# A state scan written as 64 explicit steps over 2048 columns, in place of a scan instruction over rows of time

## The reference

```python
delta = jax.nn.softplus(jnp.einsum('blr,dr->bld', delta_lo, dt_proj_w) + dt_proj_b)
A = -jnp.exp(A_log)
...
def step(h, inp):
    dt, bt, ct, xt = inp
    dA = jnp.exp(dt[..., None] * A)
    h = dA * h + dt[..., None] * bt[:, None, :] * xt[..., None]
    y = jnp.einsum('mdn,mn->md', h, ct)
    return (h, y)
h0 = jnp.zeros((M, Dm, STATE), dtype=x.dtype)
_, ys = jax.lax.scan(step, h0, (dt_seq, b_seq, c_seq, x_seq))
...
return jnp.einsum('bld,od->blo', y + x * D, out_proj_w)
```

## Time and profile before

| | us |
|---|---|
| median of 3 runs (lowest, highest) | 1664.71 (1663.49, 1667.7) |
| span of the profiled execution | 1666.7 |
| preparation of the scan stage | 1016.6 to 1069.0 of the span |
| the 32 units and the last projection | 1069.0 to 1517.2 |
| stage f and the store | 1517.4 to 1666.7 |

### The profile page before, as it was taken

The page is one execution under the profiler, slowest core; times in us unless marked ns, Lnnn a source line. Parts: engine busy times, 40 slices in busy tenths (PEclk is TensorE's granted clock), DMA queues, the critical chain, the costliest instruction groups (busy, mean ns, idle before and its releaser), DMA issues.

```text
span 1666.7 us, 41395 instructions
## 1 busy us (share of the span) xinstructions
PE 1383.1 (83%) x16240; PEld 952.6 (57%) x16240; DVE 1227.1 (74%) x2009; ACT 988.0 (59%) x2218; POOL 488.0 (29%) x423
## 2 busy tenths in 40 slices
PE   4889995799999987889999997477777777876998
PEld 2667773344444435566666774365566666664676
DVE  5787766777777747886674544699999999995533
ACT  4667672276666675766674444666666666652433
POOL 2756656712221004745551004304410000000000
PEclk8999998699999998999999999678877878776999
DMA  4100000000000001000000000201000000000000
GB/s 139 59 18 1 0 1 1 1 1 2 1 0 1 1 1 39 31 34 0 0 1 1 1 0 19 76 3 41 19 26 4 3 4 4 3 3 1 1 0 25
DMA packets 21070, 23.56 MB, mean 14 GB/s; under 512 B 2880, under 2 KB 15696, under 8 KB 20560
## 3 DMA queue, kind: packets, MB, share of 16 engines
q1 hardware_dynamic: 20912, 21.25, 4.0%
HBM read 17.04 MB, written 4.19 MB: 13 GB/s over the span
## 4 chain that ended last, share of the span: by engine, by line
PE 56%; DVE 20%; issue 12%; ACT 8%; POOL 2%; DVEq 0%; SPq 0%; DMA 0%; ACTq 0%; POOLq 0%
PE ps L517 12%; PE ps L770 7%; PE ps L594 7%; PE ps L604 7%; PE ps L801 6%; PE ps L709 4%; PE ps L672 4%; DVE arena L1643 3%; PE ps L692 3%; DVE maxima L1565 3%; DVE arena L1629 2%; DVE xn L1366 2%; ACT hr L951 2%; ACT arena L951 1%; PE ps L645 1%
## 5 line engine op out<-in xcount | busy, mean ns | idle before, releaser
L1055 ACT ACTIVATE arena<-ps,arate 128x128 f32<-128x128 f32 x1024 | 285.3, 383 | 143.5 <-PE ps L770 73.8
L1643 DVE TENSOR_TENSOR_SCAN arena<-arena 128x2048 f32<-128x2048 f32 x64 | 286.0, 4468 | 1.1
L801 PE MATMUL ps<-arena 128*32 128x32 f32 x8192 | 167.0, 236 | 82.8 <-DVE arena L1643 57.9
L1565 DVE TENSOR_REDUCE maxima<-ps 128x1 f32<-128x512 f32 (+3 forms) x320 | 190.4, 634 | 59.1 <-PE ps L675 40.0
L770 PE MATMUL ps<-arena 128*128 (+1 forms) x2048 | 203.1, 255 | 30.9 <-issue 15.5
L517 PE MATMUL ps<-xp,wup 128*128 128x512 f32 (+1 forms) x768 | 206.1, 415 | 13.7 <-ACT hr L951 10.0
L517 PE MATMUL ps<-hr,wdn 128*128 128x512 f32 x768 | 200.0, 410 | 10.0 <-DVE hr L1468 7.3
L1309 POOL TENSOR_TENSOR hr<-arena,hr 128x512 fp32r<-128x512 f32 x128 | 174.7, 1371 | 91.1 <-ACT hr L951 90.6
L801 PEld LDWEIGHTS ps<-arena 128*32 128x32 f32 x8192 | 129.6, 133 | 118.0 <-DVE arena L1643 61.2
L1468 DVE TENSOR_TENSOR hr<-arena,hr 128x512 fp32r<-128x512 f32 x128 | 126.4, 1001 | 91.0 <-ACT hr L951 89.1
L1017 ACT ACTIVATE arena<-ps 128x1024 f32<-128x1024 f32 (+1 forms) x192 | 150.4, 812 | 71.5 <-PE ps L692 37.0
(11 more groups left out here) (203 smaller groups left out, 1982.2 us busy)
## 6 DMA issues: line engine op xcount, KB each, us to landing
arena<-up_dram SPq DMA_DIRECT2D x16, 256.0 KB, 2.9
arena<-dn_dram SPq DMA_DIRECT2D x16, 256.0 KB, 3.2
parts_dram<-arena SPq DMA_DIRECT2D x8, 384.0 KB, 2.7
arena<-parts_dram SPq DMA_DIRECT2D x48, 64.0 KB, 2.4
arena<-up_dram SPq DMA_DIRECT2D x1, 1024.0 KB, 4.8
arena<-dn_dram SPq DMA_DIRECT2D x1, 1024.0 KB, 8.3
out_dram<-x SPq DMA_DIRECT2D x1, 1024.0 KB, 5.1
arena<-sel_dram SPq DMA_DIRECT2D x1, 768.0 KB, 5.0
```

The costliest lines, as they stand in the source:

```text
L801: mm = e.matmul(ps[32 * j:32 * j + 32, 6, rb * DQ:(rb + 1) * DQ], cz[:, t, :], h[:, :, t], start=(k == 0), stop=(k == 15), skip_group_chec ...
L1055: ins = e.activation(da[:, dq % 2, r * TR:(r + 1) * TR], ps[:, n % 2, j * TR:(j + 1) * TR], ACT.Exp, scale=arate[:, dq * DQ + r:dq * DQ + ...
L1565: e.tensor_reduce(maxf[:, at_max[0]:at_max[-1] + 1:max(1, at_max[-1] - at_max[0])], ps[:, n % 2, 0:ng * w].rearrange("p (g k) -> p g k", g ...
L1643: ins = e.tensor_tensor_scan(hs[:, par, part], da[:, par, part], hs[:, par, part], 0.0, ALU.mult, ALU.add)
```

## The change

The state is kept for all chunks and channels at once: a partition is still (batch row, state), and the free axis is (16 chunks, 128 channels), W = 2048 columns. The 64 steps of a chunk are walked one by one. In step t:

- TensorE writes the inputs of all columns into PSUM banks 0 to 3: 16 matmuls of 12 rows by 128 columns (`inputs`), an outer product of the bf16 parts of B and u. It also forms four banks of dt times exp(A_log), 8 matmuls of 12 rows by 64 columns each (`spread_bank`), one unit of four steps ahead;
- ScalarE takes `Exp` of each bank, 512 columns in one activation, and writes them with the time index innermost in the reading order, 2048 elements apart in the target (`decay_bank`);
- VectorE multiplies half of the state by the decay (1024 columns, `decay_state`), GpSimd the other half in two pieces of 512, and VectorE adds the inputs from PSUM (1024, 512 and 512 columns, `add_input`);
- TensorE contracts with C, 16 matmuls of 32 weight columns by 128 moving columns (`state_out`).

The scan instruction, the multiplication by B on VectorE and `arate` are gone. All of dt, u and B are now split and sent to DRAM before the steps begin (`store_dt`, `store_u`, `store_b`), and fetched by eighths (`fetch`). The fetched parts use the room of the weights of the relu mixtures, which are loaded a second time near the end of the steps. C is placed by ScalarE, A_log is exponentiated in the attention stage, and y is projected once, after the last step. The loops of the stage are unrolled.

```diff
+                def fetch(k):
+                    for c0, na in RUNS:
+                        for r in range(RG):
+                            rows = slice(32 * r + 2 * c0, 32 * r + 2 * c0 + 2 * na)
+                            sp.dma_start(dtsf[k % 2][rows], scratch["dt"][k, 0:na, :, GD * r:GD * (r + 1)].rearrange(
+                                "a b d n -> (a b) (d n)")).then_inc(dt_in[k % 2], 16)
...
+                sp.wait_ge(SC["u_split"], 4)
+                store_u(0)
+                sp.wait_ge(parts_out, 16 * (2 * NC + 3))
+                fetch(0)
+                for k in range(1, NC):
+                    store_dt(k)
+                    store_u(k)
+                sp.wait_ge(parts_out, 16 * 5 * NC)
+                fetch(1)
...
+        def spread_bank(e, n):
...
+            if q == 0 and th == 0:
+                e.wait_ge(dt_in[k % 2], 16 * KR * (k // 2 + 1))
+            if n >= 2:
+                e.wait_ge(SC["decay_ready"], n - 1)
+            for j in range(DBK):
+                mm = e.matmul(ps[:, 4 + n % 2, j * 64:(j + 1) * 64], aw[32 * r:32 * r + KR, g0 + j, :],
+                              dts[k % 2][32 * r:32 * r + KR, g0 + j, :, th * TU:(th + 1) * TU], start=True, stop=True)
...
+            for t in range(NSTEP):
+                todo = [n for n in range(ahead, ahead + (5 if t < 4 else 4)) if n < NUN * BKU]
+                ahead += len(todo)
+                for n in todo[0:1]:
+                    spread_bank(e, n)
+                if t + 1 < NSTEP:
+                    e.wait_ge(SC["added"], 3 * t + 1)
+                    inputs(e, t + 1, (0, 1))
+                for n in todo[1:2]:
+                    spread_bank(e, n)
+                if t + 1 < NSTEP:
+                    e.wait_ge(SC["added"], 3 * t + 2)
+                    inputs(e, t + 1, (2,))
+                for n in todo[2:3]:
+                    spread_bank(e, n)
+                e.wait_ge(SC["added"], 3 * t + 3)
+                if t + 1 < NSTEP:
+                    inputs(e, t + 1, (3,))
+                state_out(e, t)
+                for n in todo[3:]:
+                    spread_bank(e, n)
...
+            to = decay[:, u % 2, :].rearrange("p (t m d) -> p t m d", t=TU, d=D)[:, :, :, d0:d0 + DBK]
+            e.activation(to.rearrange("p t m d -> p d m t"),
+                         ps[:, 4 + n % 2, :].rearrange("p (d m t) -> p d m t", d=DBK, t=TU), ACT.Exp,
+                         scale=-1.0).then_inc(SC["decay_ready"], 1)
...
+                        if t >= 2 and n == 0:
+                            e.wait_ge(SC["y_done"], t - 1)
+                        e.wait_ge(SC["added"], 3 * (t - 1) + 2 + n)
+                        e.tensor_tensor(hs[:, t % 2, cols], decay[:, u % 2, t4 * W + cols.start:t4 * W + cols.stop],
+                                        hs[:, 1 - t % 2, cols], ALU.mult).then_inc(SC["pool_multiplied"], 1)
...
+                if n == 0:
+                    e.wait_ge(SC["multiplied"], t)
+                else:
+                    e.wait_ge(SC["pool_multiplied"], YP * (t - 1) + n)
+                e.tensor_tensor(to, to, of, ALU.add).then_inc(SC["added"], 1)
...
+                if t >= 2:
+                    e.wait_ge(SC["y_done"], t - 1)
+                e.wait_ge(SC["added"], 3 * (t - 1) + 1)
+                e.tensor_tensor(hs[:, t % 2, 0:HALF], decay[:, u % 2, t4 * W:t4 * W + HALF], hs[:, 1 - t % 2, 0:HALF],
+                                ALU.mult).then_inc(SC["multiplied"], 1)
...
+                for t in range(1, NSTEP):
+                    add_input(t, 0)
+                    add_input(t, 1)
+                    if t + 1 < NSTEP:
+                        decay_state(t + 1)
+                    add_input(t, 2)
```

More of the change, by code:

```diff
@@ L45 @@
 RMS_EPS = 1e-6
[L46 to L51, removed]
+NM = S // CHUNK
+NSTEP = CHUNK
+TU = 4
+TC = 8
+NC = NSTEP // TC
+NUN = NSTEP // TU
+W = NM * D
+HALF = W // 2
+RG = 4
+KR = 12
+RUNS = ((0, 3), (3, 2), (5, 1))
+GD = D // RG
+DBK = 512 // (NM * TU)
+BKU = D // DBK
+NPART = 3
+YP = 2
 ARENA = 164 * 256
@@ L188, in build @@
[L188 to L197, removed]
@@ new lines, in inputs @@
+        def inputs(e, t, banks):
+            k = t // TC
+            if t % TC == 0 and 0 in banks:
+                e.wait_ge(u_in[k % 2], 16 * KR * (k // 2 + 1))
+                e.wait_ge(b_in[k % 2], 16 * KR * (k // 2 + 1))
+            for mm_ in range(4):
+                for r in banks:
+                    rows = slice(32 * r, 32 * r + KR)
+                    mm = e.matmul(ps[:, r, mm_ * D:(mm_ + 1) * D], bs[k % 2][rows, mm_, t % TC, :],
+                                  us[k % 2][rows, mm_, t % TC, :], start=True, stop=True)
+            mm.then_inc(SC["in_done"], 1)
@@ new lines, in state_out @@
+        def state_out(e, t):
+            u, t4 = t // TU, t % TU
+            if t4 == 0:
+                e.wait_ge(SC["c_placed"], 2 * u + 2)
+                if u >= 2:
+                    e.wait_ge(SC["yT_ready"], u - 1)
+            for mh in range(4):
+                for ml in range(4):
+                    m = 4 * mh + ml
+                    mm = e.matmul(ps[32 * ml:32 * ml + 32, 6 + u % 2, 0:D], cz[:, u % 2, ml, (4 * mh + t4) * 32:(4 * mh + t4 + 1) * 32],
+                                  hs[:, t % 2, m * D:(m + 1) * D], start=(t4 == 0 and mh == 0),
+                                  stop=(t4 == 3 and mh == 3), skip_group_check=True)
+            mm.then_inc(SC["y_done"], 1)
@@ L899, in run_stages @@
+            state_turn(e, NUN - 1)
+            e.wait_ge(SC["yT_ready"], NUN)
+            for i in range(NT):
+                mm = e.matmul(ps[:, i // TPB, i % TPB * P:(i % TPB + 1) * P], yT[:, i * P:(i + 1) * P], opw[:],
+                              start=True, stop=True)
+                if i % TPB == TPB - 1:
+                    mm.then_inc(SC["proj_done"], 1)
         def run_stages(e, attention, scan, gelu_mixture, relu_mixture):
@@ L1039, in attention_scalar @@
             e.sem_inc(AT["exp_done"], 2)
+            e.activation(alog[:], alog[:], ACT.Exp).then_inc(alog_exp, 1)
             def go(items, u, par, at, first=False):
```

584 lines of the change are left out of this document (296 added, 288 removed).

## The result

The changed kernel takes 1650.3 us (median of 4 runs, 1646.4 to 1653.7) where the kernel before took 1666.2 in the same session: a ratio of 0.989, 95% interval 0.985 to 0.993. It is faster, by 16 us; the forecast was 142 us and a range that ended at 1592. The profiled execution has a span of 1651.6 us.

A forecast was written before the change was run, and what follows sets the result against it. VectorE was taken to bound the scan stage. Start 1092, steps 268, stall 7 and end 8 gave 1375 against 1517.4, 142 us less: 1524 of span, 1522 us forecast, range 1496 to 1592.

The forecast's parts named there:

- TensorE per step, at full clock: In each step, inputs, spreads, state_out and shape changes on TensorE were to take 3.9 us, as much as VectorE.
- rival 3: In the steps, TensorE at half clock: 5.9 to 8.5 us a step, 1695 us at 7.0; chance 0.07.
- The value taken, 0.63 us for 512 columns: ScalarE's decay activations from PSUM in each step: 0.63 us each, no penalty for the scattered store.
- Rival 2: ScalarE's scattered store in the steps: about 1.06 us an activation, 4.6 us a step, 1544 us; chance 0.15.
- The loops of 4.1 us: Three loops in each step, by shared port, VectorE and TensorE, each about 4.1 us; meshing them was taken as 4.25.
- The floor of 3.93: VectorE's four instructions of a step summed, with 0.03 us from one to the next: at least 3.93 us.
- Rival 1: Shared port out of phase: VectorE's product waits up to 1.29 us for GpSimd's, 5.2 us a step, 1582 us; chance 0.12.
- rule on two SBUF inputs: A VectorE instruction with two SBUF inputs and a GpSimd one reading SBUF exclude each other for a whole instruction.
- The start: Preparation before the steps: first VectorE product near 1092, steps starting 23 us later than the units did.
- The 0.45 us an issue: SyncE's time to issue one transfer in the preparation: 0.45 us, so 16.2 us for the first fetch's 36.
- The stall: In step 3, bank 32 waits for the second eighth of dt behind 21 stores: 7 us.
- The end: After the steps: state_out, copies, turn, 16 fp32 projections and the addition, 8 us.

The follow-up runs named there:

- e16: Changed kernel with its scattered store kept, GpSimd's memsets later, spreads and inputs contracting over all 128 rows: 1585.8 us.
- e1: Changed kernel with the decay activation reading PSUM in strides and storing runs of eight neighbouring elements: 1614.2 us, ratio 0.969 to the kernel before.
- e8b: Changed kernel with the dense store, later memsets, and spreads and inputs contracting over all 128 rows: 1546.8 us.
- e19: Changed kernel with dense store, later memsets, u's later stores on GpSimd behind the first spread, and a lead of 68 float32 products: 1587.4 us.
- e10: Changed kernel with dense store, later memsets and four added full-array float32 products a step, one ahead of each spread bank: 1757.3 us.
- e9: Changed kernel with the dense store and GpSimd's memsets started only after the stage's statistics: 1608.9 us.

## Why the prediction was wrong

The direction was right; the size was not, and the range missed by 58 us. The span came out at 1651.6 where the sum gave 1524: 127.6 us. It divides as follows.

- **TensorE's clock: 68 us, the step that failed.** "TensorE per step, at full clock" was taken and rival 3 given 0.07, because TensorE "has no long idle, and stayed at 1.00 (2.4 GHz) with matmuls of 8 rows". That row was one stretch of 4 us with ten matmuls; it did not stand for a stage of 12-row matmuls. e16 against the changed kernel has the clock as its main difference: 5.70 to 4.59 us over 61 steps, 68 us. Its added rows cost TensorE time of their own, so the clock's share is at least about that. Rival 3 had the mechanism and its own words for it, "only 12 of 128 rows carry data"; its price, 5.9 to 8.5 us a step, was too high: at half clock TensorE's records fill 4.7 us of a step (165.96 of 200 us at 5.70 a step, and 185.7 of 200 at 5.10 in e1). It therefore did not turn into the slower kernel that it stood for.
- **The scattered store: 44 us.** The value taken, 0.63 us for 512 columns, fell; 1.08 was measured. Rival 2 had it to 0.02 us, and e16's 4.59 is its step of 4.6. From e16 to e8b the step falls to 3.87: 0.72 x 61. With the clock at full the store alone would so have put the kernel past the forecast of 1522 but inside the range (1585.8 in the one run of e16, against 1592): it is the clock that carried it out. The rule on 16-byte lines of the Trainium skill ("SBUF — State Buffer", "Door 1: The DMA port swizzle") agrees in direction: here each element is a new line, 1.08 us, and the same elements stored in runs of eight take 0.60.
- **The loops of 4.1 us: 23 us too many.** Without clock and scatter a step is 3.87, not 4.25, and three of four take 3.47. The floor of 3.93 summed durations and added 0.03 between them; in the trace the next instruction starts 0.08 before the row of the last one ends (1.22 us from 1252.98, the next at 1254.12). Rival 1 did not happen but once a run: the first product takes 1.98 us (1119.65), as GpSimd's had started at 1119.28. From then on VectorE's is some 0.04 us ahead, as at 1270.85 against 1270.89; it takes 1.21 to 1.24 us, and GpSimd's first one waits instead (2.31 us, its second 1.24). Of the two durations that the prediction gave for its rule on two SBUF inputs, the 0.98 us was such a product; the 1.26 us was a cast with one input.
- **The start: 28 us.** Products from 1119.7, not 1092. The split of u was priced to end at 1067.3 and ended near 1081.6, with 8.25 us under the memsets, and TensorE's B products (6.3 us) at a granted clock of 0.57. The 16 stores of B were not in the sum at all: they hold SyncE until 1084.0, 2.4 us beyond the split. The first fetch starts 22 us later than forecast (1093.0, not 1071). The 0.45 us an issue was too high for the fetches (0.3) and far too low for the stores (1.4 for each of B's). Some 3 us more are the scattered store again, in the first 16 activations: from first spread to first product it is 17.5 us, and 14.1 in e1.
- **The stall: 11 us more.** Seen in the right place, step 3, but of 18 us where 7 were taken; the 21 stores were given 9 us of SyncE and hold it for 38 (1104.6 to 1142.7). In e19 the wait is 1 us.
- The end (13.7 us from the last product to stage f, 12.5 taken) and stage f (148.6, 149.3) hold: together under 1 us.

68 + 44 - 23 + 28 + 11 + 0.5 is 128.5, within 1 us of the 127.6. The two largest terms are two rivals that were listed, each by itself and at 0.07 and 0.15, and priced each on top of the forecast. Together they were never priced. Both came true, and they nearly add: the clock is worth 1.11 us a step beside the scattered store (5.70 to 4.59) and 1.23 beside the dense one (5.10 to 3.87). TensorE fills two PSUM banks that ScalarE empties, so that slow spreads and slow stores lie behind each other, as the chain above shows them by turns.

## What to carry to other kernels

Before a stage of matmuls with few rows is priced at full clock, look for a row of the same rows and density that held it: a few instructions at 1.00 prove nothing about hundreds. Choose the layout so that an activation writes densely and takes its stride on the PSUM side. Count every store of a staging pattern on the queue that also carries the fetch, by the duration of its own shape, and keep background stores behind the first fetch.

## What was not expected of the hardware

- Work of TensorE on 12 or 32 of 128 rows did not keep the granted clock at 2.4 GHz, though with four full products a step TensorE's records filled 200.00 of 200 us in e10; the same products on 128 rows did, at 169 of 200 us busy. The Trainium skill, "TensorE: Matmul & The Clock Gate", "Part 1: The HAM clock gate", lets the clock follow how busy TensorE has recently been. By busy time alone the trace disagrees, and the measurement decides.
- Two memsets in a row on GpSimd (5.22 and 3.51 us) held a VectorE operation of 16 columns for 8.25 us (0.17 in e9), past the end of the first and to the end of the second.
- Reading PSUM in strides cost ScalarE nothing that shows: 0.60 us for 512 columns in e1, 0.63 for those of L951.
- Issuing a store of 8 partitions by 48 runs took SyncE 1.4 us (22.15 us for sixteen) and GpSimd 0.73 us (10.26 us for fourteen in e19).
